# K and Q turned through memory in attention, slot rows turned by VectorE and raw expert weights asked for in halves, in a fused attention and mixture-of-experts layer

## The chip, the cores and the metric

One core of one Trainium2 chip. The metric is the device time of the whole kernel in microseconds, median of several executions.

## The reference

x is 4 x 512 tokens of 512 channels. The layer computes q, k and v for 16 heads of 128, normalises q and k by their root mean square (weights per channel), takes causal scores with a linear distance bias per head, softmax, the product with v, another RMS norm, the projection back to 512 channels, and a layer norm over x plus that. Then each token goes to the best two of 8 experts: the router's top two logits give softmax weights, each expert computes `square(relu(x w_fc)) w_proj` with 512 hidden channels, the two results are summed with their weights, and a last layer norm over the sum with its input gives the output. All in float32.

```
q, k, v = x @ Wq, x @ Wk, x @ Wv                       # 16 heads of 128
q, k = rmsnorm(q, q_rms_w), rmsnorm(k, k_rms_w)
scores = q k^T / sqrt(128) - dist * slope, causal
y = rmsnorm(softmax(scores) v, subln_w) @ Wproj
x1 = layernorm(x + y)
top_vals, top_idx = top_k(x1 @ w_router, 2); probs = softmax(top_vals)
out = layernorm(x1 + sum over the two of probs * (square(relu(x1 @ w_fc[e])) @ w_proj[e]))
```

## The kernel before, in words

Most products are made from two parts: a rounded one (`_hi`, written by ScalarE) and the remainder (`_lo`, by VectorE, GpSimd for most expert weights); TensorE multiplies hi by hi, hi by lo and lo by hi, so a product over 512 channels is 12 matmuls of 128 rows and 512 columns.

**Attention** (`attention_phase`, L102) has 16 iterations: 4 groups of 4 heads by 4 batches. An iteration has four steps i = 0 to 3, one for each tile of 128 queries; step i attends to i + 1 tiles of keys, so scores, exponentials and their transposes have width 128 (i + 1). In a step TensorE (`body`, L679) works through four heads: `score` writes one shared bank `score_ps`, VectorE's `logits` (L557) adds the bias and takes the extreme, ScalarE's `softmax` (L347) exponentiates, TensorE's `turn_probs` (L705) transposes, ScalarE copies (L354), and `attend` (L712) multiplies with v. Between these stand fillers: the projections of the next tile (`project`, L631), 12 matmuls of K after the first score, 12 of Q after the second, and 12 of V in three parts of 4. K and Q of that tile are squared by ScalarE (L269), summed per head by VectorE (`row_means`, L443), brought to a power of -1/2 by GpSimd (`rstd`, L413) and scaled into `kn` and `q_store` by VectorE (`normalise`, L447); TensorE turns each with four transposes (`turn`, L636) into `kt_ps` and `out_first`, which ScalarE rounds (L284, L291) and VectorE splits (L478, L466). In step 0 of an iteration the scores use unsplit copies (`kt_first`, L472; `qt_first`). The y of a step is normalised (L452) in the following step. Each of 3 steps splits one weight block of the next group (L607).

The order on each engine is the order of the calls written out in its `body`; there is no planner. SyncE's queue issues, per step, the next x tile (L241), y's store to `y_scratch` (L215) and clears of the slot arrays with zeros (L248, L250, 768 KB), and once per iteration three weight blocks (L222). The last step also loads y blocks (`load_blocks`, L84), the last projection weights (L228) and what routing needs (L1824, L1827).

**Routing** (`route_*`, L896 to L1294) makes, tile by tile, the projection of y, the residual and layer norm, the router, and sends each token's row by indirect DMAs to two rows of `slots_x`. y is turned there without TensorE: loading in blocks of 32 rows puts the 32 x 32 blocks in place, and VectorE's transpose (L1025) turns each.

**Experts** (`slots_*`, L1359 to L1762): 39 tiles of slot rows, in `slot_step` for most. Each is loaded (L1367), turned by four TensorE transposes (`turn_x`, L1681, L1684), rounded and split (L1499, L1561), multiplied with w_fc (`up`, L1700), rectified (L1504), squared (L1566), turned (L1708), rounded and split (L1508, L1570), multiplied with w_proj (`down`, L1711), scaled (L1514) and stored. TensorE's order in a step: turn hidden k, up k + 1, turn x k + 2, down k. Experts' weights: GpSimd asks for 2 MB raw (L1422) and 2 MB into `w_hi` (L1428), after waiting `down_done` for the block's last user, then splits eight blocks (L1437). There are three places in `w_hi` and one in `w_raw`. At the end GpSimd gathers each token's two results (L1467, 32 indirect DMAs), each after the slot tile it needs is stored (L1463), and the last layer norm follows.

Of the kernel before, what the change touches and what calls it, by code (L numbers as in the profile page):

```python
# [19 lines left out]
P = 128  # L20
QB = 4
# [62 lines left out]
def load_blocks(sp, dst, y_scratch, tile, done):  # L84

    for b in range(QB):
        at = tile * (QB * (NHG + 1)) + b * (NHG + 1) + 1
        rows = y_scratch[at:at + NHG, :, :] if isinstance(tile, int) else y_scratch[bass.ds(at, NHG), :, :]
        sp.dma_start(dst[b * QP:(b + 1) * QP, :, :].rearrange("p g (a c) -> p (g a) c", a=QB),
                     rows.rearrange("g (a j) c -> j (g a) c", a=QB)).then_inc(done, 16)  # L90
# [11 lines left out]
def attention_phase(nc, sem, x_t, w_all, qk_w, consts, y_scratch, ident, w_raw, w_hi, w_lo, early_loaded, subln_d, subln, yn,  # L102
# [6 lines left out]
    x_raw, kn, q_store, ksq, qsq = kept  # L109
# [3 lines left out]
    with ctx:  # L113
# [15 lines left out]
        ysq = sb("ysq", [P, HG, D + 1])  # L129
        qn, qt_first = q_store[:, 0:GW], q_store[:, P:P + GW].rearrange("p (h t) -> p h t", h=HG)  # L130
# [35 lines left out]
        k_first_kept = sem("k_first_kept")  # L166
        y_stored = [sem("y_stored0"), sem("y_stored1")]
        set_up, scale_set, biases_set = sem("set_up"), sem("scale_set"), sem("biases_set")
# [11 lines left out]
        def raw_block(it, m):  # L180
            return ((it + 1) % 2) * CT + m

# [5 lines left out]
        last_block = (CT - 1, 0, 1, 2)  # L188

        @block.sync  # L190
        def _(sp):
# [21 lines left out]

            def store_y(n, b):
                sp.dma_start(y_scratch[bass.ds(piece(n), QB, NHG + 1), :, :].rearrange("b t c -> t b c"),  # L215
                             yn[:, b, :].rearrange("p (b c) -> p b c", b=QB)).then_inc(y_stored[b], 16)

            def body(it, last):


                sp.wait_ge(w_ready, it * 3 + 3 * (CT - 1) + 1)
                sp.dma_start(w_raw[:, bass.ds(raw_block(it, 0), 3), :].rearrange("p m j -> p (m j)"),  # L222
                             rows_of(w_all[bass.ds(it + CT, 1), :, :])).then_inc(w_loaded, 16)
                for i in range(TB):
                    if last:

                        sp.wait_ge(w_ready, last_it * 3 + 3 * CT + i)
                        sp.dma_start(w_raw[:, last_block[i], :], w_last[:, i, :]).then_inc(wp_loaded, 16)  # L228
                    if last and i == TB - 1:
                        sp.wait_ge(q_summed, its * TB)  # L230
                        sp.wait_ge(q_turned, its * TB)
                        load_first_x(sp)
                        load_route_consts(sp)
                    if last and i == 1:


                        sp.wait_ge(y_stored[1], 16 * (((NHG - 1) * NT + 1) // 2 + 2))
                        load_blocks(sp, w_raw[:, CT:2 * CT, :], y_scratch, 0, early_loaded)
                    if not last:
                        sp.wait_ge(x_ready, it * TB + i + 3)  # L240
                        sp.dma_start(x_raw[:, i % 2, :], rows_of(x_t[bass.ds((it * TB + i + 4) % NT, 1), :, :]))\  # L241
                            .then_inc(x_loaded[i % 2], 16)
                    sp.wait_ge(y_normed, it * TB + i + 1)
# [7 lines left out]
                        .then_inc(y_cleared, 16)  # L251

# [13 lines left out]
        def _(act):  # L266
            def square(out, src, projected, count, done):
                act.wait_ge(projected, count)
                nc.scalar.activation(out[:, :, 0:D], src[:, :].rearrange("p (h d) -> p h d", h=HG), ACT.Square,  # L269
                                     scale=float(D) ** -0.5).then_inc(done, 1)  # L270

            def square_y(count):
                if count is not None:
                    act.wait_ge(y_done, count)
                nc.scalar.activation(ysq[:, :, 0:D].rearrange("p h (b i) -> p b h i", b=QB), block_columns(y_ps[:, :]),
# [6 lines left out]
            def round_k(parity, i, count):  # L282
# [3 lines left out]
                    kt_ps[:, :].rearrange("p (h t) -> p h t", h=HG), ACT.Copy).then_inc(k_rounded, 1)  # L286

            def round_q(i, count):
                act.wait_ge(q_turned, count)
                out = qt_first if i == 0 else qt_hi[:, :, :]  # L290
                nc.scalar.activation(out, qt_ps[:, :].rearrange("p (h t) -> p h t", h=HG),  # L291
# [26 lines left out]
            for sq in (ksq, qsq):  # L318
                nc.scalar.activation(sq[:, :, D], half[:, :], ACT.Copy, scale=-2 * EPS).then_inc(set_up, 1)
            round_x(0, 16)  # L320
            round_first(*FIRST[0])
            square(ksq, k_ps, k_projected, 1, k_squared)
            round_first(*FIRST[1])
            round_first(*FIRST[2], 0, 1)
            square(qsq, q_ps, q_projected, 1, q_squared)
# [1584 lines left out]
```

## Time and profile before

| | us |
|---|---|
| median of 3 runs | 1440.74 (1440.17 to 1444.86) |
| the profiled execution | 1442.51 |
| its span | 1440.7 |
| TensorE busy | 1400.9 (97%) |
| VectorE busy | 813.3 (56%) |
| ScalarE busy | 730.3 (51%) |
| GpSimd busy | 424.2 (29%) |

Busy is the union of an engine's instructions; PE is TensorE, DVE VectorE, ACT ScalarE, POOL GpSimd, SP SyncE. Matmuls overlap: what one costs is the distance from its start to that of the next, not its duration. The granted clock of TensorE is 0.992 of full speed over the span.

### The profile page before, as it was taken

The numbers are of one execution on the slowest core, as the hardware profiler recorded it, in microseconds if no ns is written. First come the engines' busy times: TensorE is split into PE (matmuls) and PEld (weight loads), VectorE is DVE, ScalarE is ACT, GpSimd is POOL, SyncE is SP. The second block draws the span as 40 slices with busy tenths as digits, with TensorE's granted clock in tenths as the row PEclk, the third lists the DMA queues.
The fourth block names the chain that finished last, engine by engine and source line by source line (L and its number), as shares of the span: only waits on it lengthen the run. The fifth ranks groups of instructions, "written<-read, shape, count | busy, mean of one in ns | idle before, by whom it ended". The sixth has DMA issues, their size and how long they took to land. (4 is left out here: it accounts for less than half of the span.)

```text
span 1440.7 us, 26432 instructions
## 1 busy us (share of the span) xinstructions
PE 1400.9 (97%) x7744; PEld 1184.6 (82%) x7745; DVE 813.3 (56%) x1877; ACT 730.3 (51%) x1633; POOL 424.2 (29%) x410
## 2 busy tenths in 40 slices
PE   8999999999999999999999999999999989999994
PEld 6888888888888888888888888878887868888783
DVE  6555655656556555555565555567777763333334
ACT  5565656656556566566565565543333223333334
POOL 1212221212112122222121212103445553353565
PEclk9999999999999999999999999999999999999997
DMA  5243333232433333333334245557659546756699
GB/s 185 75 130 95 109 95 115 88 113 91 131 95 109 95 96 108 96 107 109 117 89 115 76 128 157 143 136 171 148 137 233 176 139 247 265 201 230 187 192 237
DMA packets 136851, 200.45 MB, mean 139 GB/s; under 512 B 16624, under 2 KB 83312, under 8 KB 133488
## 3 DMA queue, kind: packets, MB, share of 16 engines
q1 hardware_dynamic: 126032, 149.67, 36.0%
q0 software_dynamic: 10784, 50.36, 11.9%
q8 instruction: 17, 0.28, 0.1%
q14 instruction: 18, 0.15, 0.0%
HBM read 160.05 MB, written 92.62 MB: 175 GB/s over the span
## 5 line engine op out<-in xcount | busy, mean ns | idle before, releaser
L413 POOL TENSOR_TENSOR small<-small,half 128x4 f32<-128x4 f32 x193 | 195.0, 1010 | 764.2 <-DVE small L443 764.2
L557 DVE CUSTOM_DVE_ANT_0 logit<-score_ps,bias 128x128 f32<-128x128 f32 (+3 forms) x256 | 124.8, 487 | 157.1 <-PE score_ps L699 117.6
L347 ACT ACTIVATE prob<-logit,small 128x128 f32<-128x128 f32 (+3 forms) x256 | 144.2, 563 | 120.1 <-DVE small L557 116.5
L712 PEld LDWEIGHTS y_ps<-vs,prob_t 128*128 128x128 f32 x1280 | 175.1, 191 | 21.5 <-ACT prob_t L354 4.5
L712 PE MATMUL y_ps<-vs,prob_t 128*128 (+1 forms) x1280 | 185.6, 276 | 0.7 <-ACT prob_t L354 0.7
L354 ACT ACTIVATE prob_t<-prob_ps 128x128 f32<-128x128 f32 (+3 forms) x256 | 111.5, 436 | 54.9 <-PE prob_ps L705 53.9
L705 PE MATMUL prob_ps<-ident,prob 128*128 128x128 f32 x640 | 112.8, 274 | 3.2 <-ACT prob L347 2.8
L443 DVE TENSOR_REDUCE small<-squares 128x4 f32<-128x516 f32 x128 | 88.4, 691 | 45.7 <-ACT squares L269 43.8
L631 PE MATMUL v_ps<-w_hi,x_hi 128*128 (+1 forms) x256 | 106.7, 417 | 1.4 <-DVE w_lo L488 1.4
L929 ACT ACTIVATE yt_hi<-x_raw,subln 128x512 fp32r<-128x512 f32 x60 | 43.2, 723 | 126.2 <-DVE x_raw L1025 51.2
L631 PE MATMUL v_ps<-w_hi,x_lo 128*128 (+1 forms) x256 | 106.6, 416 | 0.0
L631 PE MATMUL k_ps<-w_hi,x_hi 128*128 (+1 forms) x256 | 102.8, 402 | 0.8 <-DVE w_lo L488 0.8
L631 PE MATMUL v_ps<-w_lo,x_hi 128*128 (+1 forms) x256 | 102.8, 402 | 0.0
L631 PE MATMUL q_ps<-w_hi,x_hi 128*128 (+1 forms) x256 | 101.9, 398 | 0.8 <-DVE w_lo L488 0.8
L631 PE MATMUL k_ps<-w_hi,x_lo 128*128 (+1 forms) x256 | 100.9, 394 | 0.0
L631 PE MATMUL q_ps<-w_hi,x_lo 128*128 (+1 forms) x256 | 100.9, 394 | 0.0
L631 PE MATMUL k_ps<-w_lo,x_hi 128*128 (+1 forms) x256 | 100.7, 393 | 0.0
L631 PE MATMUL q_ps<-w_lo,x_hi 128*128 (+1 forms) x256 | 100.5, 393 | 0.0
L1437 POOL TENSOR_TENSOR w_lo<-w_raw,w_hi 128x512 f32 (+1 forms) x56 | 74.6, 1367 | 85.4 <-DMA w_hi<-in_w_experts 81.2
L705 PEld LDWEIGHTS prob_ps<-ident,prob 128*128 128x128 f32 x640 | 80.0, 142 | 13.8 <-ACT prob L347 6.9
L452 DVE TENSOR_TENSOR x_now<-y_ps,small 128x512 f32<-128x512 f32 x65 | 45.0, 692 | 77.5 <-POOL small L413 77.5
L269 ACT ACTIVATE squares<-k_ps 128x512 f32<-128x512 f32 x64 | 38.3, 599 | 94.3 <-PE k_ps L631 94.3
(233 smaller groups left out, 3370.0 us busy)
## 6 DMA issues: line engine op xcount, KB each, us to landing
slots_x<-in_zeros SPq DMA_DIRECT2D x64, 512.0 KB, 4.4
y_scratch<-x_now SPq DMA_DIRECT2D x65, 256.0 KB, 2.8
x_raw<-in_x_t SPq DMA_DIRECT2D x64, 256.0 KB, 2.6
slots_y<-in_zeros SPq DMA_DIRECT2D x64, 256.0 KB, 4.4
y_raw<-y_scratch SPq DMA_DIRECT2D x56, 256.0 KB
w_raw<-in_w_experts POOLq DMA_DIRECT2D x7, 2048.0 KB
w_hi<-in_w_experts POOLq DMA_DIRECT2D x7, 2048.0 KB
w_raw<-in_w_all SPq DMA_DIRECT2D x16, 768.0 KB, 6.1
```

Source lines behind the costliest of these rows:

```text
L269: nc.scalar.activation(out[:, :, 0:D], src[:, :].rearrange("p (h d) -> p h d", h=HG), ACT.Square, scale=float(D) ** -0.5).then_inc(done, 1)
L347: nc.scalar.activation(prob[:, 0:width], logit[:, 0:width], ACT.Exp, scale=-1.0, bias=least[:, h:h + 1], accum_out=row_sum[:, (i % 2) * HG ...
L354: nc.scalar.activation(prob_t[:, 0:width], prob_ps[:, 0:width], ACT.Copy)\
L413: nc.gpsimd.tensor_tensor(r, ms, half[:, :], ALU.pow).then_inc(ready, 1)
L443: nc.vector.tensor_reduce(ms, sq[:, :, :], AX.X, ALU.add).then_inc(done, 1)
L452: nc.vector.tensor_tensor(block_columns(out), block_columns(y_ps[:, :]), y_r.unsqueeze(1).unsqueeze(3).to_broadcast([P, QB, HG, QP]), ALU. ...
L557: nc.vector.tensor_tensor_reduce(out=logit[:, 0:width], in0=score_ps[:, 0:width], in1=bias[:, h, T - width:T], scale=1.0, scalar=3e38, op0 ...
L631: mm = nc.tensor.matmul(out[:, :], xs, ws, start=(s == 0), stop=(s == 3 * CT - 1))
L705: mm = nc.tensor.transpose(prob_ps[:, j * P:(j + 1) * P], prob[:, j * P:(j + 1) * P], ident[:, :])
L712: mm = nc.tensor.matmul(y_ps[:, :].rearrange("p (b h i) -> p h b i", b=QB, h=HG)[:, h, :, :], prob_t[:, j * P:(j + 1) * P], one(vs[:, bass ...
L929: nc.scalar.activation(yt_hi[:, g, :], turned[g % 2], ACT.Copy, scale=subln[:, 0:1])\
L1437: nc.gpsimd.tensor_tensor(lo, w_raw[:, s, :], hi, ALU.subtract).then_inc(we_split, 1)
```

## The change

In attention, each tile's projections are made two steps ahead instead of one (the first two tiles before the loop). VectorE scales K and Q into one tile `kq` (`normalise_part`), SyncE stores it to `kq_scratch` at the end of a step (`store_kq`) and loads it back at the start of the next with four DMAs, one for each block of 32 partitions (`load_kq`), and VectorE turns K and Q from it (`turn_part`) after the logits of the third head. The result lies in SBUF, in free blocks of `w_raw`, from which ScalarE rounds and VectorE splits. TensorE's eight transposes go, for all tiles but the first. The fillers now hold 12 matmuls of K, 6 and 6 of Q, 9 and 3 of V. One buffer `sq` holds the squares of K, Q and y in turn. The weights of the next group are loaded a step before their iteration and split in steps 1 and 2. In the last iteration the products of y with the projection weights are spread over two steps.

In the experts, slot rows are loaded in four blocks (for one tile two of them by ScalarE's queue), six tiles ahead, and VectorE turns them (`turn_x`) into the two `x_raw` halves; TensorE's transposes go, and w_fc's rows are ordered on the host to fit. `round_x` and `split_x` of a tile stand ahead of `rectify` and `square`. Raw weights come in two halves: the first and the `w_hi` load are issued after the fourth of eight splits, the second after the eighth. Before the first `up` after the tables, 46 filling transposes stand for 10.

```
+            def store_kq(t):
+                sp.wait_ge(k_normed, t + 1)
+                sp.wait_ge(q_normed, t + 1)
+                ...
+                    sp.wait_ge(kq_loaded, (t - 1) * (16 * QB))
+                sp.dma_start(kq_scratch, kq[:, :]).then_inc(kq_stored, 16)
+            def load_kq(t):
+                sp.wait_ge(kq_stored, t * 16)
+                sp.nop(nofuse=True)
+                sp.wait_ge(k_turned, t)
+                sp.wait_ge(q_turned, t)
+                rows = kq_scratch.rearrange("(a j) (b c) -> b j a c", a=QB, b=QB)
+                for b in range(QB):
+                    sp.dma_start(kq_in[b * QP:(b + 1) * QP, :].rearrange("p (a c) -> p a c", a=QB), rows[b])\
+                        .then_inc(kq_loaded, 16)
             def body(it, last):        # SyncE
-                sp.wait_ge(w_ready, it * 3 + 3 * (CT - 1) + 1)
-                sp.dma_start(w_raw[:, bass.ds(raw_block(it, 0), 3), :].rearrange("p m j -> p (m j)"),
...
                 for i in range(TB):
+                        load_kq(it * TB + i + 1)
...
+                    if not last and i == TB - 1:
+                        load_w(it + 1)
                     sp.wait_ge(y_normed, it * TB + i + 1)
                     store_y(it * TB + i, i % 2)
...
+                    if not (last and i >= TB - 2):
+                        store_kq(it * TB + i + 2)
```

VectorE's step:

```
                     logits(0)
-                    row_means(ysq, y_ms, y_squared, n + 1, y_summed)
+                    row_means(y_sq, y_ms, y_squared, n + 1, y_summed)
                     normalise_y(yn[:, i % 2, :], n + 1)
-                        row_means(ksq, k_ms, k_squared, n + 2, k_summed)
                     logits(1)
-                        normalise(kn[:, :], k_ps, k_r, k_rstd, n + 2, k_normed)
-                        split_x(i % 2, n + 3)
-                        row_means(qsq, q_ms, q_squared, n + 2, q_summed)
+                        row_means(kq_sq, k_ms, k_squared, n + 3, k_summed)
+                    if i in (1, 2):
+                        split_w(i - 1)
                     logits(2)
-                        normalise(qn[:, :], q_ps, q_r, q_rstd, n + 2, q_normed)
+                    if i == 2:
+                        split_w(2)
+                        turn_part(1, kt, n + 1, k_ready, k_turned)
+                        turn_part(0, qt, n + 1, q_ready, q_turned)
+                        normalise_part(1, k_ps, k_r, k_rstd, n + 3, k_normed)
                     logits(3)
+                        row_means(kq_sq, q_ms, q_squared, n + 3, q_summed)
                         if nxt_i == 0:
-                            keep_first_k(n + 2)
-                        split_k(nxt, nxt_i, n + 2)
-                        split_q(nxt_i, n + 2)
+                            keep_first_k(n + 2, kt)
+                        split_k(nxt, nxt_i, n + 2, kt)
+                        split_q(nxt_i, n + 2, qt)
+                        split_x((i + 1) % 2, n + 4)
+                        normalise_part(0, q_ps, q_r, q_rstd, n + 3, q_normed)
```

The experts:

```
+            def split_turn(e, ahead, end):     # GpSimd
+                pool.wait_ge(raw_half[0], 16 * e)
+                pool.wait_ge(we_cast, 16 * e)
                 for s in range(WT):
+                    if s == WT // 2:
+                            pool.wait_ge(raw_half[1], 16 * e - 16)
                     nc.gpsimd.tensor_tensor(lo, w_raw[:, s, :], hi, ALU.subtract).then_inc(we_split, 1)
+                    if s == WT // 2 - 1 and ahead is not None:
+                        load_raw_half(nxt, 0)
+                            pool.wait_ge(down_done, end)
+                        load_rounded(ahead, nxt)
+                load_raw_half(nxt, 1)
...
             def slot_step(k, b, h, y, q):      # VectorE
                 split_hid(b, k)
+                if more(k, 2):
+                    split_x(b, k + 3)
                 if more(k, 1):
                     square(1 - b, k + 2)
-                if more(k, 2):
-                    split_x(b, k + 3)
+                if more(k, 3):
+                    turn_x(1 - b, (y + 3) % YB, (q + 1 + (y + 3) // YB) * (16 * QB), k + 2)
...
             def slot_step(k, b, h, y, q):      # TensorE
                 turn_hid(b, k)
                 if more(k, 1):
                     up(1 - b, load_owner(k + 1), k + 2)
-                if more(k, 2):
-                    turn_x(b, h * 16 + 32)
                 down(b, load_owner(k), k)
```


## Rows read from the trace of the kernel before

**Rows 1.** the page: busy us, share of the span, instructions

```profile
PE 1400.9 (97%) x7744; PEld 1184.6 (82%) x7745; DVE 813.3 (56%) x1877; ACT 730.3 (51%) x1633; POOL 424.2 (29%) x410
```

**Rows 2.** busy PE, PEld, DVE, ACT, POOL; clock, DMA share, GB/s: attention, experts

```profile
22.00:930.00 908.00, 901.55 (x5275) 779.60 (x5274) 520.60 (x1125) 538.92 (x1294) 189.46 (x188) 1.00 0.36 109
...
1182.00:1408.00 226.00, 224.66 (x1099) 183.21 (x1100) 75.83 (x103) 77.56 (x137) 112.98 (x89) 0.99 0.70 217
```

**Rows 3.** same columns, steps 0 to 3 of an iteration

```profile
487.59:499.72 12.13, 11.89 (x66) 9.77 (x65) 7.16 (x18) 7.22 (x21) 3.02 (x3) 1.00 0.32 87
499.72:512.97 13.25, 13.25 (x80) 11.62 (x81) 8.20 (x19) 8.13 (x22) 3.02 (x3) 1.00 0.37 118
512.97:528.41 15.44, 15.44 (x96) 13.76 (x95) 9.09 (x19) 9.61 (x22) 3.02 (x3) 1.00 0.29 85
528.41:545.50 17.09, 17.09 (x104) 14.77 (x104) 8.49 (x17) 9.54 (x21) 3.02 (x3) 1.00 0.39 123
```

**Rows 4.** waits in attention: total us, times, longest

```profile
PE score_ps L699 <- DVE qt_lo L466: 3.4, 15, 0.2
```

**Rows 5.** waits in the experts, same columns

```profile
POOL w_lo L1437 <- DMA w_hi<-in_w_experts: 81.2, 6, 15.1
```

**Rows 6.** TensorE's timeline in step 1, around both turns: start, us, instruction

```profile
507.26 0.60 PE L636 MATMUL kt_ps<-ident,kn 128*128 128x128 f32 x4
507.62 0.47 PE L631 MATMUL v_ps<-w_hi,x_hi 128*128 x1
...
510.58 0.60 PE L636 MATMUL out_first<-ident,q_store 128*128 128x128 f32 x4
511.01 0.61 PE L712 MATMUL y_ps<-vs,prob_t 128*128 x4
```

**Rows 7.** VectorE's timeline in step 0

```profile
490.37 0.69 DVE L452 TENSOR_TENSOR x_now<-y_ps,small 128x512 f32<-128x512 f32 x1 [1.19 <-POOL small L413]
...
496.38 0.69 DVE L447 TENSOR_TENSOR q_store<-q_ps,small 128x512 f32<-128x512 f32 x1 [0.91 <-POOL small L413]
496.99 0.28 DVE L557 CUSTOM_DVE_ANT_0 logit<-score_ps,bias 128x128 f32<-128x128 f32 x1
```

**Rows 8.** VectorE's groups: busy us, mean ns, idle before

```profile
L1025 DVE STREAM_TRANSPOSE x_raw<-y_raw 128x512 f32<-128x512 f32 x56 | 39.5, 706 | 0.9 <-DMA y_raw<-y_scratch 0.3
...
L1566 DVE TENSOR_TENSOR y_raw<-kn 128x512 f32<-128x512 f32 x39 | 35.1, 900 | 74.6 <-ACT kn L1504 68.7 <-issue 5.9
```

**Rows 9.** DMA issues: count, KB each, median us from issue to landing

```profile
slots_x<-in_zeros SPq DMA_DIRECT2D x64, 512.0 KB, 4.4
y_scratch<-x_now SPq DMA_DIRECT2D x65, 256.0 KB, 2.8
x_raw<-in_x_t SPq DMA_DIRECT2D x64, 256.0 KB, 2.6
...
slots_y<-y_raw SPq DMA_DIRECT2D x39, 256.0 KB, 2.2
...
w_raw<-y_scratch SPq DMA_DIRECT2D x8, 256.0 KB, 6.0
```

**Rows 10.** SyncE's queue in step 2: start, us of the issue

```profile
520.51 0.35 SPq L241 DMA_DIRECT2D x_raw<-in_x_t  x1
```

**Rows 11.** timeline of one expert tile, all engines

```profile
1264.11 0.60 PE L1684 MATMUL turn_ps<-ident,y_raw 128*128 128x128 f32 x4
1264.31 0.60 ACT L1504 ACTIVATE kn<-turn_ps 128x512 f32<-128x512 f32 x1 [2.06 <-PE turn_ps L1693]
...
1264.94 1.67 DVE L1566 TENSOR_TENSOR y_raw<-kn 128x512 f32<-128x512 f32 x1 [1.97 <-ACT kn L1504]
...
1270.60 0.60 PE L1684 MATMUL turn_ps<-ident,y_raw 128*128 128x128 f32 x4
```

**Rows 12.** GpSimd's timeline, the first two of the last 16 gathers

```profile
1395.30 1.56 POOL L1467 DMA_INDIRECT x<-slots_y,slot_y  x1 [4.38 <-DMA slots_y<-y_raw]
1397.16 1.55 POOL L1467 DMA_INDIRECT x<-slots_y,slot_y  x1 [0.30 <-issue]
```

More of the change, by code:

```diff
@@ L224, in body @@
                 for i in range(TB):
-                    if last:
+                    if last and i == TB - 1:
+                        sp.wait_ge(k_ready, its * TB)
+                        sp.wait_ge(q_ready, its * TB)
+                        load_blocks(sp, w_raw[:, CT:2 * CT, :], y_scratch, 0, early_loaded, NHG - 1, NHG)
+                        sp.dma_start(w_raw[:, last_block[i], :], w_last[:, i, :]).then_inc(wp_loaded, 16)
+                    else:
+                        load_kq(it * TB + i + 1)
@@ L342, in body @@
                     nxt, nxt_i = (it % 2, i + 1) if i < TB - 1 else ((it + 1) % 2, 0)
+                    far, far_i = (it % 2, i + 2) if i < TB - 2 else ((it + 1) % 2, i + 2 - TB)
                     ahead = not (last and i == TB - 1)
+                    projects = not (last and i >= TB - 2)
                     def softmax(h):
@@ L424, in body @@
                     rstd_y(it * TB + i + 1)
-                    if not (last and i == TB - 1):
-                        rstd_kq(it * TB + i + 2)
+                    if not (last and i >= TB - 2):
+                        rstd_kq(it * TB + i + 3)
             nc.gpsimd.memset(logit[:, 0:P], 0.0).then_inc(fill_set, 1)
@@ L552, in body, with split_w @@
                     ahead = not (last and i == TB - 1)
+                    projects = not (last and i >= TB - 2)
+                    def split_w(at):
+                        m = W_ORDER[at]
+                        dve.wait_ge(w_rounded, it * 3 + 3 * CT + at + 1)
+                        blk = w_block((hg + 1) % 2, m, b)
+                        nc.vector.tensor_tensor(
+                            one(w_lo[:, bass.ds(blk, 1), :]), w_raw[:, m, :],
+                            one(w_hi[:, bass.ds(blk, 1), :]), ALU.subtract).then_inc(w_ready, 1)
                     def logits(h):
@@ L577, in body @@
-                    if not (last and i >= 2):
-                        split_x(i % 2, n + 3)
-                    if ahead:
-                        row_means(qsq, q_ms, q_squared, n + 2, q_summed)
-                    logits(2)
-                    if ahead:
-                        normalise(qn[:, :], q_ps, q_r, q_rstd, n + 2, q_normed)
-                    else:
-                        split_y(2)
+                    if last and i == TB - 2:
+                        dve.wait_ge(early_loaded, 16 + 32 * QB)
+                        turn_y(2)
```

463 lines of the change are left out of this document (274 added, 189 removed).

## The prediction

> **What bounds the kernel now.** I read the engines' shares first: TensorE is busy 97% of the span [rows 1]. The stages then say where: attention (about 22 to 930 us) and the experts (1182 to 1408) have almost no TensorE gap, at a granted clock of 1.00 and 0.99; DMA is about a third busy in the one, 0.70 in the other [rows 2]. So a TensorE instruction taken out there is worth its pitch, provided that nothing put in its place ends later. One attention iteration of four steps takes 12.13, 13.25, 15.44 and 17.09 us; VectorE is busy in 50 to 62% of each [rows 3]. The waits show no step in which TensorE stands long: the largest of its own are 3.4 us in all, for qt_lo [rows 4]. In the experts TensorE never appears as waiting for a weight split, though GpSimd waits 81 us for weights [rows 5].
>
> **Attention: what goes.** Per step, four transposes of K (0.36 us from the first to the next matmul) and four of Q (0.43 us to the next) [rows 6]: 0.8 us. The first tile keeps its own, so 63 steps lose them: 50 us at most. The first step of an iteration ends in a 0.23 us wait for qt_lo, in 15 places [rows 4]; its work now lies a step earlier and it goes too: per iteration 4 x 0.8 + 0.2 = 3.4 us. New TensorE steps: 11.1, 12.45, 14.65 and 16.3 us.
>
> **Fillers.** The 36 projection matmuls of a step, 0.23 us each, stay; between the four heads they stand 12, 6, 6, 9, 3, where 12, 12, 4, 4, 4 plus the turns stood. Shortest cover: probabilities of head 1 in step 0. Its transposes now come 5.0 us into the step. The logits follow the y normalisation, which ends 3.5 us in [rows 3, 7]; add 0.4 for logits, then about 0.7 for the exponential: 4.7. Covered by 0.3; I cost it at nothing, and at 0.3 us in every fourth step (5 us) if that cover is gone. ScalarE's squares now share one buffer, so each waits for VectorE's previous sum; those sums end 2 us or more earlier. Head 3 has the chain below.
>
> **Attention: what comes.** K and Q of the tile after next are normalised into one tile, stored (512 KB), loaded back by four DMAs of 128 KB, turned by two VectorE transposes (0.706 us in that form [rows 8], of which the next operation overlaps some 0.08, as in [rows 7]: 0.63 each), rounded and split. That adds 1.3 us to VectorE's 7.2 to 9.1 per step: 8.4 of 11.1 at the most crowded, so it doesn't bound by share. It does by order, because the transposes stand before logits of head 3, and the normalisation of Q that feeds the next store stands last. That closes a loop over steps: turn K, turn Q, normalise K (1.9 us), logits of head 3 (0.3), row sum (0.6), split K (0.6), split Q after ScalarE's rounding (0.8), split x (0.6), normalise Q (0.65), in all about 5.5 us; then the round trip R through memory, and the next step's turns.
>
> R is not in the trace; its parts have neighbours [rows 9]. The store: a 256 KB store to memory lands in 2.2, 256 KB in short pieces in 2.8, a 512 KB clear with another behind it in 4.4. I take 3.5, ends 2.9 and 4.4. The load: x's 256 KB lands in 2.6; four 256 KB loads of y blocks land in 6.0. Mine moves half of that in a quarter of the pieces, issues 0.35 to 0.4 us apart [rows 10]: 1.2 for the issues and 2.5 for the last, 3.7; ends 3.4 and 6.0. Semaphores and SyncE's register work before the two issues: 0.5 (0.3 to 0.6). R = 7.7, ends 6.6 and 11.
>
> Now walk. In step 3 TensorE scores head 3 by 11.5, logits end at 12.6, then row sum, first K, split K, split x and Q follow: normalised 15.65 us in, so K and Q arrive 0.65 before its end plus R: 7.05 us into step 0. VectorE would be ready at 5.85 (logits of head 2), so it stands 1.2; logits of head 3 end at 9.2, the split of Q at 11.25: 0.15 lost. Q of that step is normalised 1.2 us into step 1, so arrival there is 8.9, where VectorE is ready at 7.0; exponential of head 3 at 12.0 instead of 11.2, split of Q at 13.4 to 13.5: 1.05 lost. In step 2 arrival is 8.8 against 8.55, in step 3 before need: nothing. Loss 1.2 per iteration, net 3.4 - 1.2 = 2.2, over 15.75 iterations **35 us**. With R = 7.0 the loss is 0.2 (gain 50); each further us of R costs about 2 us per iteration, because two links of the loop lie bare; at 8.7 the gain is gone; at 11, adding 2.3 us of R at 2.3, the loss exceeds it by 5.3 (-83 us).
>
> What is queued behind the new waits: on SyncE, x, y's store and both clears stand behind the load's wait for the store. x is asked for a step ahead and y has two buffers, so 5 us of lateness are free; the clears (768 KB) are issued about 6 us into the step and have landed before the next store at 12. The w load (768 KB) comes in step 3 and is used 11 us later, in the next step: hidden. Traffic rises from about 104 GB/s, the mean of the steps [rows 3], by 1 MB per 13.7 us to near 180; the experts already move 217 [rows 2].
>
> The Trainium skill ("DMA: Bandwidth & Descriptors", Anatomy of one DMA) puts one transfer at about 2.0 us plus its bytes over 436 GB/s. That would make the store 3.2 and the last load 2.3, R = 7.2, and the sum some 10 us lower; its fit is for the GpSimd queue, and the rows for 512 KB lie above it.
>
> **Experts.** Each tile takes 6.49 us [rows 11]; the x turn takes 0.36 plus 0.08 of slower start behind it, 0.44, times 37 tiles: **16 us**. VectorE's transpose and the split from memory instead of PSUM lie off TensorE's path: the hidden square, queued behind the split of x, needs to be done when down ends, 2.8 us after up; rectify and square take 1.3 of it [rows 11]. Rows are loaded six tiles ahead. Raw weights in halves: worth nothing, since no TensorE wait stood on weights [rows 5]. GpSimd's wait for down_done moves between the fourth and fifth split; behind it stand four splits (5.3 us) that TensorE needs only an expert (some 30 us) later. The last split now waits for TensorE and moves with it. The end: 16 gathers at 1.85 us run unbroken from 1395.3 after a 4.4 us wait for stored rows, the last of four such waits of 12.8 us in all [rows 12]; earlier rows start them earlier, so the tail follows.
>
> **Seams.** First rows and tile 2's rows now take four DMAs and a 0.7 us transpose where four 0.09 us transposes stood: +0.5 each, less two turns off TensorE: 0. Start, filled with tile 1's projections, and the shifted y projection: 0, within 3 us.
>
> **Sum.** The profiled execution took 1442.5 (span 1440.7): 1442.5 - 35 - 16 = 1391.5. It stood 1.8 above the median of the runs: **1390**.
>
> **Rivals.**
> (a) The round trip hides (R 7.0 or less): attention gains 50 to 53.5, time 1372. For: 2.2 us for a 256 KB store. Against: 4.4 for 512 KB. The Trainium skill's fit above would put R nearly here. Chance 0.27.
> (b) R 8.2 to 9.2: attention gives 17 to -17, time 1408 to 1442, middle 1425. Or the thinner fillers bare softmax by 0.3 to 0.5 us a step (20 to 30 us): same range. For: SyncE issues everything in order. Chance 0.17.
> (c) Slower: the memory loop becomes the bound of every step. Place: VectorE standing before the K turn, in steps 0 to 2. Price 2 to 3 us per us of R per iteration; it decides from R = 9.3, where attention loses the 16 us of the experts. At R = 10, 1390 + 35 + 3.1 x 15.75 = 1474. For: the y block loads' 6.0 us. Against: their bytes. Chance 0.09.
> (d) Experts give nothing: VectorE operations with all operands in SBUF sometimes take 1.67 instead of 0.69 us while GpSimd splits weights (mean 0.90) [rows 8, 11]; there are now three such per tile instead of one. 3 us more on VectorE per tile during splits, about 13 tiles, could bare 1 us each: 1403. The Trainium skill ("SBUF — State Buffer", SBUF: two separate sides) says the pair of ports shared by VectorE and GpSimd is an exclusive lock, which speaks against putting this work there. Chance 0.1.
> (e) The transposes are gone but their time isn't, because TensorE waits at the next step's k_ready in the same places: no change, 1437 to 1445. Chance 0.02.
>
> **How the numbers follow.** My forecast has 0.35; its own range is 1380 to 1402 (R 7.3 to 8.1, seams 3). The range for 8 in 10 reaches over (a), (d) and most of (b): 1368 to 1428. A measurement here can tell about 0.3% (4 us). Slower: (c), 0.09. Same: (e) and the edge of (b), 0.03. Faster: 0.88.
>
> **What would show it.** No kt or qt transposes but four each; matmul pitch 0.23 us unchanged. VectorE idle before the K turn, released by the load, about 1 us in step 0, 2 in step 1, none in step 3: that fixes R. Iterations of 55.7 us. Expert tiles of 6.05 us. TensorE waits on probabilities of head 3 or on qt_lo in steps 0 and 1 only. I am wrong if the store plus the load takes over 8.2 or under 7.2 us, if TensorE waits at heads 0 to 2, or if tiles of experts stay above 6.2.

## The result and the profile after

| | before | after |
|---|---|---|
| median, us | 1441.83 (4 runs, 1440.17 to 1444.86) | 1469.47 (4 runs, 1465.65 to 1469.98) |
| profiled span | 1440.7 | 1464.0 |
| TensorE busy | 1400.9 | 1368.1 |
| TensorE gaps (span less busy) | 39.8 | 95.9 |

The ratio is 1.018, 95% interval 1.016 to 1.021: slower by 28 us, where 1390 was forecast. TensorE lost 33 us of work and gained 56 us of gaps. The page's line of shares, which answers to [rows 1]:

```profile
PE 1368.1 (93%) x7120; PEld 1131.0 (77%) x7121; DVE 922.9 (63%) x2042; ACT 721.7 (49%) x1632; POOL 458.7 (31%) x416
```

I cut each profile at the same five marks: the last product of probabilities and v in attention, the first `up` of an expert, the fourth `up` (the steady run of tiles begins), the end of the last `down`, the end of the span. Each number is a stage's length in us, from the start times of those matmuls. The last rows are kernels of the experiments below.

| | attention | routing | first three tiles | other 36 | tail | span |
|---|---|---|---|---|---|---|
| before | 956.3 | 199.5 | 26.3 | 242.3 | 16.3 | 1440.7 |
| after | 966.5 | 204.6 | 34.0 | 241.6 | 17.3 | 1464.0 |
| split_early | 921.3 | 205.2 | 34.0 | 244.2 | 20.0 | 1424.7 |
| attn_only | 971.8 | 204.3 | 26.3 | 239.4 | 17.2 | 1459.0 |
| whole_raw | 965.3 | 206.5 | 30.7 | 226.1 | 23.1 | 1451.7 |
| cast_after | 966.9 | 204.3 | 33.5 | 225.4 | 18.1 | 1448.2 |
| raw_ahead | 966.4 | 204.1 | 33.5 | 241.7 | 18.7 | 1464.4 |
| early_cast | 919.6 | 208.0 | 33.4 | 225.5 | 18.2 | 1404.7 |
| all_three | 918.2 | 205.6 | 30.8 | 227.2 | 18.1 | 1399.9 |

**Attention.** The windows of the four steps of one iteration after the change, and of the third step of the next iteration, with the columns of [rows 3]:

```profile
501.72:512.42 10.70, 10.70 (x58) 8.86 (x57) 7.49 (x20) 7.06 (x21) 3.40 (x3) 1.00 0.67 209
512.42:524.91 12.49, 12.49 (x75) 10.73 (x74) 8.93 (x21) 8.80 (x22) 3.78 (x3) 1.00 0.59 189
524.91:543.70 18.79, 16.73 (x87) 14.02 (x86) 11.18 (x23) 8.71 (x20) 3.77 (x3) 0.91 0.40 126
543.70:560.53 16.83, 16.83 (x99) 14.30 (x98) 9.32 (x19) 9.47 (x20) 3.13 (x3) 1.00 0.61 194
583.72:600.96 17.24, 15.16 (x87) 12.62 (x86) 11.19 (x23) 8.72 (x20) 3.78 (x3) 1.00 0.41 137
```

Against the forecast of 11.1, 12.45, 14.65 and 16.3 us, steps 0, 1 and 3 (10.70, 12.49, 16.83) are about right. The third is not: 18.79 us, or 17.24 in the next iteration, against 15.44 before [rows 3]. The waits of attention (engine, line, released by: total us, times, longest) say what is late:

```profile
PE q_ps L719 <- DVE w_lo L633: 30.9, 15, 2.1
DVE w_raw L516 <- DMA kq_in<-kq_scratch: 23.3, 16, 7.3
```

Fifteen times, 2.06 us each: TensorE stands ahead of the projection of Q for `w_lo`, the second weight split of the next group. The loop through memory, which I had feared, makes VectorE wait 23.3 us in 16 places, of which 7.3 lie in one place in the last iteration. There TensorE stands 5.3 us behind it (for `prob_t`); at the other 15 it has no wait of this kind. TensorE's timeline in that third step (start, us, instruction, idle before and releaser):

```profile
529.25 0.33 PE L794 MATMUL score_ps<-kt_hi,qt_lo 128*128 x1
531.64 0.49 PE L719 MATMUL q_ps<-w_hi,x_hi 128*128 x1 [2.06 <-DVE w_lo L633]
531.97 0.40 PE L719 MATMUL q_ps<-w_lo,x_hi 128*128 x1
532.20 0.60 PE L719 MATMUL q_ps<-w_hi,x_lo 128*128 x1
532.60 0.63 PE L719 MATMUL q_ps<-w_hi,x_hi 128*128 x1
533.03 0.63 PE L719 MATMUL q_ps<-w_lo,x_hi 128*128 x1
```

and VectorE's:

```profile
529.73 0.56 DVE L640 CUSTOM_DVE_ANT_0 logit<-score_ps,bias 128x384 f32<-128x384 f32 x1 [0.85 <-PE score_ps L794]
...
530.21 0.69 DVE L498 TENSOR_REDUCE small<-sq 128x4 f32<-128x516 f32 x1
530.81 0.68 DVE L633 TENSOR_TENSOR w_lo<-w_raw,w_hi 128x512 f32 x1
```

The split stands behind the logits of the second head (529.73) and the row sum of K (530.21), and TensorE can't go on to its next fillers, the projection of Q, until it is done (531.5). The logits of a head can't be earlier than that head's scores, which end at 529.6, so the wait, as written, is built into the two orders. In this iteration the distance from one matmul to the next then goes from 0.23 us to 0.40 and 0.43 (531.97 to 533.03): TensorE's granted clock is at the lower of its two levels, 1.2 instead of 2.4 GHz, for 3.4 us, after a 2.06 us pause, and the mean of the 18.79 us is 0.91. Of the 14 iterations behind the first, seven have that and take 58.8 us; the other seven 57.3 (third step 17.24, clock 1.00).

The code shows one thing more. TensorE's wait for that split is written for step 2 of every iteration, but what an iteration splits is used from the next group on, and the projection reads it in the same iteration only in the last iteration of a group: 3 of the 15 times. In the other 12 the wait asks for a count and not for data that is needed. A kernel with the wait in those three alone was not run.

**Experts.** An undisturbed tile takes 6.06 us, as forecast (6.05). But where one expert ends and GpSimd is released, a tile takes 8.7 to 8.9 us (8.3 at the first) and the next often 6.4 to 7.6. There, GpSimd's timeline and VectorE's:

```profile
1285.18 0.53 POOL L1542 DMA_DIRECT2D w_hi<-in_w_experts  x1 [17.47 <-PE router_ps L1841]
1285.73 5.02 POOL L1559 TENSOR_TENSOR w_lo<-w_raw,w_hi 128x512 f32 x4
```

```profile
1285.64 0.69 DVE L1716 TENSOR_TENSOR yt_lo<-out_first,yt_hi 128x512 fp32r<-128x512 f32 x1 [2.08 <-ACT yt_hi L1641]
1286.24 5.07 DVE L1701 TENSOR_TENSOR yt_lo<-x_raw,yt_hi 128x512 fp32r<-128x512 f32 x1
1291.23 0.68 DVE L1712 TENSOR_TENSOR y_raw<-kq 128x512 f32<-128x512 f32 x1
```

The split of the token rows (L1701, all operands in SBUF since the turn moved to VectorE) takes 5.07 us instead of 0.68 and ends 0.6 us behind GpSimd's burst of four weight splits (1290.75); the square that TensorE waits for (1291.23) stands behind it. It is so at five tiles, with 4.78 to 5.07 us, and in the first three tiles a square takes 5.74. The square of 5.74 us even starts before the burst does, inside the issue ahead of it, and is held all the same. GpSimd, then VectorE:

```profile
1198.05 0.58 POOL L1542 DMA_DIRECT2D w_hi<-in_w_experts  x1
1198.62 4.94 POOL L1559 TENSOR_TENSOR w_lo<-w_raw,w_hi 128x512 fp32r<-128x512 f32 x4
```

```profile
1198.38 5.74 DVE L1712 TENSOR_TENSOR y_raw<-kq 128x512 f32<-128x512 f32 x1 [3.33 <-ACT kq L1637]
```

In the kernel before, the same split read PSUM, and of the two only the square read SBUF alone (at most 1.8 us; one of 1.67 stands in [rows 11]).

### The profile page after: what moved, and what is told of

It is laid out like the page before. It is cut to its first block and busy times, and to the rows that moved or that the text cites. A ratio compares the mean times of both kernels' runs of the same rounds, so it can differ in the third digit from the quotient of the medians.

```text
span 1464.0 us, 27019 instructions
## 1 busy us (share of the span) xinstructions
PE 1368.1 (93%) x7120; PEld 1131.0 (77%) x7121; DVE 922.9 (63%) x2042; ACT 721.7 (49%) x1632; POOL 458.7 (31%) x416
## 5 line engine op out<-in xcount | busy, mean ns | idle before, releaser
L467 POOL TENSOR_TENSOR small<-small,half 128x4 f32<-128x4 f32 x193 | 225.8, 1170 | 746.6 <-DVE small L498 746.6
L807 PEld LDWEIGHTS y_ps<-vs,prob_t 128*128 128x128 f32 x1280 | 182.1, 195 | 43.0 <-ACT prob_t L404 22.3
L807 PE MATMUL y_ps<-vs,prob_t 128*128 (+1 forms) x1280 | 193.1, 283 | 6.1 <-ACT prob_t L404 6.0
L719 PE MATMUL q_ps<-w_hi,x_hi 128*128 (+1 forms) x256 | 108.4, 424 | 31.6 <-DVE w_lo L633 30.9
L498 DVE TENSOR_REDUCE small<-sq 128x4 f32<-128x516 f32 x193 | 132.4, 686 | 5.7 <-ACT sq L312 5.6
L719 PE MATMUL q_ps<-w_hi,x_lo 128*128 (+1 forms) x256 | 105.2, 411 | 0.0
L719 PE MATMUL q_ps<-w_lo,x_hi 128*128 (+1 forms) x256 | 104.1, 406 | 0.0
L719 PE MATMUL v_ps<-w_hi,x_lo 128*128 (+1 forms) x256 | 101.5, 397 | 0.0
L516 DVE STREAM_TRANSPOSE w_raw<-kq_in 128x512 f32<-128x512 f32 x126 | 82.0, 690 | 24.6 <-DMA kq_in<-kq_scratch 23.5
L719 PEld LDWEIGHTS q_ps<-w_hi,x_hi 128*128 128x128 f32 x256 | 49.9, 195 | 44.0 <-issue 35.6
```

The costliest lines, as they stand in the source:

```text
L467: nc.gpsimd.tensor_tensor(r, ms, half[:, :], ALU.pow).then_inc(ready, 1)
L498: nc.vector.tensor_reduce(ms, terms, AX.X, ALU.add).then_inc(done, 1)
L516: nc.vector.transpose(turned_columns(out), in_parts[:, m]).then_inc(done, 1)
L719: mm = nc.tensor.matmul(out[:, :], xs, ws, start=(s == 0), stop=(s == 3 * CT - 1))
L807: mm = nc.tensor.matmul(y_ps[:, :].rearrange("p (b h i) -> p h b i", b=QB, h=HG)[:, h, :, :], prob_t[:, j * P:(j + 1) * P], one(vs[:, bass ...
```

## The experiments

Each recorded expectation defines its own letters; C and D don't mean the same in all of them. Theories at this point. **A**: the late weight split costs attention about 43 us. **B**, its rival: the loop through memory sets the pitch. **For the experts**: C, GpSimd beside all-SBUF instructions costs wherever they stand; F, it is the place of the second burst, behind the last down product; then H and J, below.

**split_early** changes only VectorE's order:

```
-                    if i in (1, 2):
-                        split_w(i - 1)
+                    if i == 1:
+                        split_w(0)
                     ...
                     logits(2)
-                    if i == 2:
-                        split_w(2)
+                    if i in (1, 2):
+                        split_w(i)
```

> Only the place of two VectorE instructions in attention is changed: the split of the next Q weights moves from behind the second head's logits of the third step to behind the third head's logits of the second step. Theory A (the late split is what makes the third step 18.8 us long): TensorE's 2.06 us wait ahead of the q projection goes in all 15 iterations (30.9 us), the half-clock stretches of 3.4 us that stood behind it go with it (7 of them, 1.7 us each, 12 us), the third step falls to 14.7 to 15.5 us and the whole to 1415 to 1432 us. Rival B (the loop through memory sets the pitch; the wait only hid it): a wait for k_ready or q_ready at a head start, or VectorE's wait for kq_in, takes its place, third step 17.5 us or more, whole 1450 to 1468 us.

Measured: 1426.74 us (1424.79 to 1427.43), ratio to before 0.991 (0.989 to 0.993): 43 us under the changed kernel, and faster than before. The third and fourth steps:

```profile
500.83:515.70 14.87, 14.87 (x87) 12.67 (x86) 10.56 (x22) 8.72 (x20) 3.40 (x3) 1.00 0.50 159
515.70:532.52 16.82, 16.82 (x100) 14.29 (x98) 9.32 (x19) 9.47 (x20) 3.14 (x3) 1.00 0.58 194
```

The third step is 14.87 us (forecast 14.65), the iteration 54.91, and no wait for `w_lo` is left in the loop. VectorE's wait for the loads shrinks with it, to 14.1 us in 17 places, 7.9 of them in one. A stands, B falls.

**store_twice**, to see how much slack the loop has once that is mended: split_early with this.

```
                 sp.dma_start(kq_scratch, kq[:, :]).then_inc(kq_stored, 16)
+                sp.wait_ge(kq_stored, t * 32 - 16)
+                sp.dma_start(kq_scratch, kq[:, :]).then_inc(kq_stored, 16)
                 ...
-                sp.wait_ge(kq_stored, t * 16)
+                sp.wait_ge(kq_stored, t * 32)
                 ...
```

> split_early with K and Q written to memory twice, the second write waiting for the first (each took 2.6 us to land), so that the loop through memory lasts about 2.6 us more, 9.9 in place of 7.3. Theory K (the prediction's: the loop has under 1 us of slack in VectorE's wait and about 2 us to the next step's head): 0.6 to 2 us per step, 60 steps, 1460 to 1540 us. Rival L (there is slack; what VectorE waits for is covered by TensorE's fillers): 1427 to 1440 us.

Measured: 1531.70 us (1531.16 to 1533.72), 105 us more. VectorE's timeline in step 0 to 1 of an iteration, first split_early, then store_twice (normalisation of Q, then the turns):

```profile
488.26 0.68 DVE L509 TENSOR_TENSOR kq<-q_ps,small 128x512 f32<-128x512 f32 x1
...
496.25 1.30 DVE L516 STREAM_TRANSPOSE w_raw<-kq_in 128x512 f32<-128x512 f32 x2 [0.36 <-DMA kq_in<-kq_scratch]
```

```profile
544.12 0.68 DVE L511 TENSOR_TENSOR kq<-q_ps,small 128x512 f32<-128x512 f32 x1
...
554.77 1.30 DVE L518 STREAM_TRANSPOSE w_raw<-kq_in 128x512 f32<-128x512 f32 x2 [3.27 <-DMA kq_in<-kq_scratch]
```

From the end of the normalisation to the landing it is 7.3 us in split_early (496.25 - 488.94) and 10.0 in store_twice (554.77 - 544.80). An iteration goes from 54.9 to 61.6 us: 6.7 us for 2.7 us more of round trip in each of four steps. So 6.7 of 10.8 us came through, which leaves about 1 us of slack a step (an estimate from these numbers). K stands, L falls.

**square_first** puts the square ahead of the split of the token rows in VectorE's `slot_step`, as before.

```
                 split_hid(b, k)
-                if more(k, 2):
-                    split_x(b, k + 3)
                 if more(k, 1):
                     square(1 - b, k + 2)
+                if more(k, 2):
+                    split_x(b, k + 3)
```

> Only the order of two VectorE instructions in an expert tile is changed: the square of the next tile's hidden rows comes ahead of the split of the token rows two tiles on, as in the kernel before. Theory C (where GpSimd splits weights, the split of the token rows takes 2.0 to 5.1 us instead of its undisturbed time, with all operands in SBUF, and stands ahead of the square that TensorE waits for): out_first and x_ps waits of TensorE on the square (14.3 us together) fall to under 8, whole 1453 to 1461 us. Rival D (the square itself is held by GpSimd, up to 5.7 us, wherever it stands): whole within 3 us of 1469.5.

Measured: 1467.54 us (1465.96 to 1469.66), no difference; tiles at an expert's end 7.7 to 7.9 us and the next 6.7 to 7.1. Now the square is held: it starts 2.6 to 2.7 us into the burst and takes 2.9 to 3.0 us, to 0.6 us behind the burst's end. C's number for this run fails, D's holds.

**attn_only** is the changed attention with the expert part of the kernel before (its turns on TensorE, its whole raw weights, its order).

> Attention of the changed kernel with the experts (TensorE turns, raw weights whole) of the kernel before. Theory C (the new expert part costs about 5 us more than the old one and the seam 3): 1460 to 1464 us, and the expert stage from its first to its last down product as long as before. Rival D (the old experts behind the new attention lose nothing and the seam nothing: all of the 8 us comes back): 1458 us or less. Rival E (the new expert part is in fact the faster one and the loss is all in attention): 1475 to 1485 us.

Measured: 1460.39 us (1459.13 to 1460.70), in C's range; D (1458 or less) and E (1475 and more) fall. The new expert part costs 9 us on balance. By the table, the first three tiles pay 7.7 of it (26.3 to 34.0), and the 36 tiles, which should have come down by 16, are 2.2 us longer than attn_only's.

**whole_raw** is the changed kernel with GpSimd's `load_turn` and `split_turn` as before: raw weights in one transfer, eight splits in one burst.

> The changed kernel with the raw expert weights asked for whole, and the splits of one expert in one go, as before; VectorE still turns the token rows. Theory C (it is GpSimd's splits beside VectorE's all-SBUF instructions that cost, wherever they stand): within 4 us of 1469.5 us. Rival F (the halves put the second four splits right behind an expert's last down product, where TensorE needs the rounded weights and the VectorE results at once): 1450 to 1460 us. If whole weights come later than the halves did and TensorE waits for them: above 1474 us.

Measured: 1454.38 us (1453.39 to 1457.52), 15 us under the changed kernel. The 36 tiles take 226.1 us, 13.3 under attn_only: nearly the forecast of 0.44 us a tile. F's number holds, but the bursts of eight still run beside VectorE's instructions, and hold none of them beyond 1.84 us, so C as it was put for this run falls. What differs, then, in the second burst of four? Place, or the transfer asked for directly ahead of it?

**cast_after** keeps the place and moves the transfer:

```
                         if end is not None:
                             pool.wait_ge(down_done, end)
                             pool.nop(nofuse=True)
-                        load_rounded(ahead, nxt)
+                if ahead is not None:
+                    load_rounded(ahead, nxt)
                 pool.wait_ge(we_split, WT * e + WT)
```

> The changed kernel (late Q split kept), with GpSimd's transfer of the next rounded weights asked for behind the second four splits, no longer ahead of them; the splits still start when an expert's last down product ends. Theory H (an asked-for or running transfer of rounded weights from GpSimd's own queue is what lets the four splits hold an all-SBUF instruction of VectorE to their end): the split of the token rows there takes under 2 us in place of 4.8 to 5.1, the tiles of 8.9 us fall to under 7, whole 1453 to 1462 us. Rival J (it is the place, the moment at which the burst of four meets VectorE's instruction): it still takes 4.8 us and more, tiles of 8.9 us stay, whole 1466 to 1475 us.

Measured: 1450.96 us (1449.10 to 1452.08). The burst and the same two VectorE instructions:

```profile
1248.85 5.95 POOL L1559 TENSOR_TENSOR w_lo<-w_raw,w_hi 128x512 f32 x4 [2.91 <-PE out_ps L1842]
```

```profile
1249.88 0.69 DVE L1717 TENSOR_TENSOR yt_lo<-x_ps,yt_hi 128x512 fp32r<-128x512 f32 x1 [2.22 <-ACT yt_hi L1642]
1250.49 1.45 DVE L1702 TENSOR_TENSOR yt_lo<-x_raw,yt_hi 128x512 fp32r<-128x512 f32 x1
1252.41 1.23 DVE L1713 TENSOR_TENSOR y_raw<-kq 128x512 f32<-128x512 f32 x1 [0.47 <-ACT kq L1638]
```

The burst starts on the same release (`down_done`), but now takes 5.95 us instead of 5.03 and lets VectorE in: 1.45 and 1.23 us. Every tile at an expert's end takes 6.1 us. H stands, J falls, and F with it: the place is the same, and the loss is gone.

**raw_ahead** asks for something else directly ahead of that burst: cast_after, with the first raw half there.

```
-                        load_raw_half(nxt, 0)
                         if end is not None:
                             pool.wait_ge(down_done, end)
                             pool.nop(nofuse=True)
+                        load_raw_half(nxt, 0)
```

> cast_after, with the first raw half asked for directly ahead of the second four splits, where the rounded weights stood in the changed kernel. Theory H1 (any transfer that GpSimd asks for directly ahead of its splits lets them hold VectorE's all-SBUF instruction to their end): the split of the token rows takes 4.5 to 5.1 us again, tiles of 8.9 us are back, whole 1464 to 1472 us. Rival H2 (only the transfer of rounded weights does it): 1.2 to 1.6 us as in cast_after, whole 1449 to 1455 us.

Measured: 1468.06 us (1464.66 to 1473.29), tiles of 8.4 us.

```profile
1251.34 0.56 POOL L1546 DMA_DIRECT2D w_raw<-in_w_experts  x1 [6.54 <-PE out_ps L1842]
1251.92 5.03 POOL L1559 TENSOR_TENSOR w_lo<-w_raw,w_hi 128x512 f32 x4
```

```profile
1252.01 0.69 DVE L1717 TENSOR_TENSOR yt_lo<-x_ps,yt_hi 128x512 fp32r<-128x512 f32 x1 [2.21 <-ACT yt_hi L1642]
1252.62 4.89 DVE L1702 TENSOR_TENSOR yt_lo<-x_raw,yt_hi 128x512 fp32r<-128x512 f32 x1
```

The split takes 4.89 us again, so a raw transfer asked for there does it as the rounding one did (H1). The split in the line above it, which reads PSUM (`x_ps`), starts in the same burst and takes its 0.69 us. A transfer under way doesn't hold anything: in cast_after a burst begins at 1224.4, some 5 us after the raw half was asked for (1219.02), which lands 11.2 us after issue in the median there, and the split beside it took 1.25 us.

All 14 kept traces, `before` among them, say the same. Bursts that begin within 0.03 us of the end of an issue of GpSimd's met a VectorE instruction with its operands in SBUF 32 times, and each was held until 0.55 to 0.56 us behind the burst's end. Beside the other bursts, whose last issue ended 1.9 us or more before, there were 274 such instructions, none longer than 1.84 us.

**early_whole, early_cast**: both repairs in one kernel, split_early with whole_raw and with cast_after.

> The changed kernel with both repairs: the split of the Q weights a step earlier, and the raw expert weights whole with all eight splits in one burst. If the two losses are independent (theory A for attention, F for the experts): 1426.7 - (1469.5 - 1454.4) = 1411.6 us, 1408 to 1415. If the earlier experts run into the gathers on GpSimd at the end (its tail was 23.2 us with whole weights, 17.3 before them): up to 1418 us. If they fed on the same time: above 1420 us.

> The two repairs together, the split of the Q weights a step earlier and the rounded weights asked for behind the second four splits, the raw halves kept. If they are independent: 1469.5 - 42.7 - 18.5 = 1408.3 us, 1405 to 1411, so 1 to 4 us under early_whole. If GpSimd's gathers at the end are what sets the time now, no gain on early_whole (1410.3).

Measured: 1410.26 (1408.88 to 1412.61) and 1406.32 us (1402.86 to 1407.04). The two losses are independent: 42.7 and 18.5 us off 1469.5 make 1408.

**blocks_late**, early_whole with SyncE's loads of y blocks in the last iteration behind that step's clears, tests why K and Q land late once (the 7.9 us above):

> As early_whole, and in the last attention iteration SyncE asks for the first blocks of Y behind the first step's clears and its store of K and Q, no longer ahead of them. Theory G (the 4.15 us of issues and the scattered blocks hold the loads of K and Q in that one step, 7.9 us of waiting for VectorE and 5.8 us for TensorE): 4 to 6 us under early_whole. Rival: the blocks now come late for VectorE's turns of Y or hold the next step's loads: within 2 us of early_whole or slower.

Measured: 1410.53 us (1406.26 to 1411.29), no difference. G falls: VectorE still waits 6.8 us. SyncE's queue in this run shows another suspect, a clear of 2304 KB, which stands between the loop and the last iteration:

```profile
861.82 0.34 SPq L224 DMA_DIRECT2D kq_scratch<-kq  x1
862.37 0.64 SPq L298 DMA_DIRECT2D slots_x<-in_zeros  x1
865.27 2.47 SPq L233 DMA_DIRECT2D kq_in<-kq_scratch  x4
```

The loads issued 2.9 us behind it land 8 us after issue instead of 2.9.

**all_three** moves that clear behind the third step of the last iteration, and asks for the first raw half of the second expert turn behind its splits (one square had taken 5.2 us there, behind such an issue).

> early_cast, with the zeroing of 2304 KB moved from ahead of the last attention iteration to behind its third step, and the first expert turn's raw transfer asked for behind its splits. Theory G2 (that zeroing, issued just ahead of the loads of K and Q, is what made them land 8.0 instead of 2.9 us after issue in that one step): TensorE's wait of 5 to 6 us in the last iteration goes, and 2 to 4 us at the start of the experts, where a square took 5.2 us: 1398 to 1403 us. Rival: the zeroing collides with the loads of the routing instead, or the raw weights come late: within 3 us of early_cast.

Measured: 1400.15 us (1398.18 to 1408.14), ratio to before 0.973 (0.970 to 0.975). The loads of the last iteration's first step land 2.6 to 3.2 us after issue, VectorE's waits for the loads in that iteration are 0.2 and 0.4 us, TensorE's longest wait for `prob_t` 1.6 instead of 5.3; the first three tiles take 30.8 instead of 33.4 us. G2 stands. (The table has only 1.4 us less in attention than early_cast: the last iteration is 6.5 us shorter, but in this execution the first scores start 1.4 us later, the first iteration takes 1.6 more and another, once, 2.2 more.) This is the fastest of the kernels that were run, by a little over early_cast:

```profile
PE 1349.6 (96%) x7120; PEld 1121.3 (80%) x7121; DVE 908.1 (65%) x2042; ACT 721.7 (52%) x1632; POOL 458.3 (33%) x416
```

**round_late**: in the first step of all, ScalarE stands for the first weight blocks ahead of its first exponential (in split_early):

```profile
37.19 0.63 ACT L409 ACTIVATE w_hi<-w_raw 128x512 f32 x1 [5.70 <-DMA w_raw<-in_w_all]
37.72 0.39 ACT L397 ACTIVATE prob<-logit,small 128x128 f32<-128x128 f32 x1
```

so in all_three the rounding of an iteration's first block is moved behind the second head's probability copy:

```
-                    if i < 2:
-                        round_w(W_ORDER[i])
+                    if i == 1:
+                        round_w(W_ORDER[1])
                     ...
                     keep_prob_t(1)
+                    if i == 0:
+                        round_w(W_ORDER[0])
```

> all_three, with ScalarE's rounding of the first weight block of an iteration moved from ahead of the first head's exponential to behind the second head's probability copy. Theory M (in the very first step ScalarE stands 5.7 us for weights that SyncE asks for at 31.1 us, ahead of the first exponential, and TensorE stands 5.0 us with it): the 5.0 us of wait shrink to at most 2, the first step falls from 18.2 us to 13 to 15 us, whole 3 to 5 us under all_three (1395 to 1397 us). Rival: the wait only moves behind the second head, or the rounding now crowds a later step of every iteration: within 2 us of all_three or slower.

Measured: ratio to before 0.972 (0.970 to 0.973), as all_three; 1405.62 us, on a chip where the kernel before took 1446.06. M and its rival both came true: the first step fell from 17.9 to 13.4 us, and each later iteration rose by 0.3 us (54.9 to 55.2), 14 times. No net gain.

## Why the prediction was wrong

**The step that failed** is the third of the "New TensorE steps", 14.65 us, which measured 17.24 and 18.79: the moved weight splits had no price in the working, so attention, which was to give 35 us, took 10 more (956.3 to 966.5). I walked VectorE's order for K, Q, x and the logits, and costed the fillers as free, but of the three splits of the next group's weights I didn't ask who waits for them in their new places. Before, TensorE asked for all three in step 3, behind the steps that made them; now its wait ahead of the projection of Q in step 2 asks for the split that VectorE makes in that same step, behind logits that can start only when TensorE has ended its scores and wants to go on (529.73 against 529.58). The price is 2.35 us in each of 14 iterations (57.26 against 54.91), 1.5 more in the seven where the clock falls, and 3.1 in the first (65.5 against 62.4): 46.5 us; from mark to mark it is 45.2. The warning "I am wrong if [...] TensorE waits at heads 0 to 2" fitted the symptom, for a cause that I had not named. The slower rival (c) named the memory loop, which was not it.

**The memory loop** was the well worked part, with some luck in it. R was 7.7, measured 7.3, but the parts miss by more: to the first load's issue it is 2.9 us (my 3.5 and 0.5 of semaphores), from there to the landing 4.4 (my 3.7). The estimate from the Trainium skill ("DMA: Bandwidth & Descriptors", Anatomy of one DMA), 2.0 us plus the bytes over 436 GB/s, gave R = 7.2. The trace agrees with its sum better than with mine, and not with its parts: 3.7 against 2.9 and 3.5 against 4.4 cancel too. "VectorE idle [...] about 1 us in step 0, 2 in step 1" was about 1 us in step 1 alone, and 0.36 in split_early, so the 1.2 us an iteration that I took off for it didn't come. "Each further us of R costs about 2 us per iteration": store_twice measured 6.7 for 2.7, 2.5 each. The fillers cost nothing, as set down: TensorE is busy all of steps 0, 1 and 3.

**The steps** with the late split mended: 10.69, 12.53, 14.87 and 16.82 us against 11.1, 12.45, 14.65 and 16.3, together 54.9 against 54.5, or against 55.7 with the waits I had set down. Attention then gains exactly the 35 us of the sum (956.3 to 921.3), but by luck, from two errors that cancel: an iteration gives 3.2 us (58.15 to 54.91, start to start) instead of 2.2, and the ends of attention take 10 back.

**Seams, "0, within 3"**: mis-sized. In split_early the first scores start 9 us later (30.1 against 21.1, one more tile projected ahead of the loop), and the first iteration takes 62.4 us with a 5.0 us wait for weights; the last one is 2.4 shorter. Routing takes 5 to 8.5 us more and the first three tiles 7 more. early_cast, with both repairs, lands at 1406 and not at 1390 for these. Part of the tiles' 7 is the held square (all_three gives back 2.6). Of routing's share the traces show a wait of 4.1 to 4.4 us at its start (1.4 before), ended by nothing but TensorE's own sequencer; why it grew was not tried.

**Experts, "0.44 us a tile, 16 us"**: right where nothing holds VectorE (6.06 us a tile; 13.9 us over 36 tiles, 239.4 to 225.5). **"Raw weights in halves: worth nothing"**: this is the second failed step. They cost 16 us (241.6 against 225.4). I had moved GpSimd's wait and its four splits and asked only when TensorE needs the weights; not what lies directly ahead of the burst on GpSimd's own queue. cast_after keeps the halves and loses nothing by them.

**Rival (d)** named the right pair of engines and the wrong size: 1 us bared in 13 tiles. Sharing alone costs up to 1.2 us an instruction, and TensorE hardly sees it (6.06 us in nearly every tile of whole_raw and cast_after); the bare part is a hold of 5 us, five or six times. The Trainium skill ("SBUF — State Buffer", Who interferes with whom) says that the second to issue blocks until the first finishes. The trace agrees where no transfer is asked for ahead: the held instruction takes at most 1.84 us beside GpSimd instructions of 1.26 to 1.5 us. Behind an asked-for transfer it is held over what is left of a burst of four, up to 5.74 us, which is more than that rule gives; the measurement decides.

The range's upper end, 1428, and the chances (0.88 for faster) were too sure: the one case of a slower kernel turned on R, the quantity that I knew to be unknown, and none on a wait that the change itself had moved.

## What to carry to other kernels

When a change shifts a pipeline by a step, list every wait of the bounding engine again and ask for each on which instruction, in its new place, it now rests; a support operation that had an iteration of room (a weight split of 0.7 us) can become the whole loss. Trace operands as well as operations: an instruction whose source moves from PSUM to SBUF becomes one that GpSimd can hold. And on GpSimd's queue, ask for transfers behind a burst of SBUF work, or some 2 us ahead of it, not directly ahead. Last, look whether a wait that costs time asks for data or only for a count.

## What was not expected of the hardware

- A VectorE instruction with its operands in SBUF that falls into a burst of four GpSimd instructions ends 0.6 us behind the whole burst (it takes 2.9 to 5.7 us by where it starts) when GpSimd asked for a transfer directly ahead of them, and takes 0.7 to 1.8 us when it didn't. The transfer may be raw or rounding. Bursts behind an issue take 4.9 to 5.04 us, the others 5.2 to 6.0. Shown by cast_after and raw_ahead; why the issue does it was not tried.
- The granted clock fell to half for 3.4 us after a 2.06 us pause of TensorE in 7 of 14 iterations that all have that pause, at 1.5 us each; what sets the seven apart was not tried. In split_early, without it, it fell in attention only behind the 5.0 us pause of the first step and the 5.8 us one of the last iteration.
- One clear of 2304 KB to memory, issued 2.9 us ahead, makes four loads of 128 KB land after 8.0 to 8.7 us instead of 2.9 (blocks_late); with the clear moved they take 2.6 to 3.2 (all_three).
